# Cross-attention and quantised FFN: ScalarE's residual moved behind the gelu, TensorE's last products by tile behind four unused products, VectorE's affine passes half a step later

## The chip, the cores and the metric

The kernel runs on one core of a Trainium2 chip. The time is the device time of one launch in microseconds (us), the median of three executions. The engines are TensorE (PE for its matmuls, PEld for its weight loads), VectorE (DVE), ScalarE (ACT), GpSimd (POOL) and SyncE (SP), which here only issues transfers. Each engine takes its own instructions in order, and they meet through semaphores.

## What is computed

```
x = x + xattn(layernorm(x), ctx) @ Wo + bo          # x: 64 batches of 256 rows, 256 wide
h = bitlinear(layernorm(x) * g1 + b1n, W1, b1)      # 256 -> 1024, input rounded to 8 bits per row
h = gelu(h)
h = layernorm(h) * g2 + b2n                         # over the 1024
x = x + bitlinear(h, W2, b2)                        # 1024 -> 256, input rounded to 8 bits per row
...
bitlinear: scale = 127 / max|row|; round(row * scale) @ ternary(W).T / scale + b
```

## The kernel before

A batch is 256 rows, two tiles (t = 0, 1) of 128 rows. The program has two parts. The first (steps of `attn`) does the attention of all 64 batches (NB = 64) and the first layernorm of the FFN; it leaves the rounded rows of every batch turned in `h_t`. The second part (steps of `ffn`) does the rest of the FFN, and it alone is touched. Each engine has a function `ffn(j, n)` of its own, written by hand, that is called for j = 0, 1, 2, ...; the steps in the middle run in a hardware loop unrolled four times. The order within each `ffn` and the semaphores are all that sets the order of the work.

What happens to batch j, tile t:

- TensorE, `rows_up` (L1233, L1238): four matmuls of 512 columns and two more for the bias fill `u_p[t]`, two of the eight PSUM banks. There is one `u_p` for each tile, so batch j+1's tile t can be made only when ScalarE (`ssq_done`) and VectorE (`g_centred`) have read batch j's.
- ScalarE, `gelu` (L1089), in place in `u_p[t]`, with the row sum; `deviation`: the negative mean `g_nm` (L1094), the last 256 columns centred into `part` (L1097), and the sum of squares through a Square over all 1024 (L1099). An instruction with a row sum is followed by a short ACTIVATION_READ_ACCUMULATOR. After both tiles come `variance` (L1105) and, for batch j-2, `step_size` (L1110).
- VectorE, `centre` (L843): the first 768 columns, centred and times the gain, into `gn`. `affine` (L857): `gn` times the row's scale plus the offset, both tiles, 1024 columns each; the offset is read from PSUM banks 0 and 1 (`b2n_p`) from batch 4 on, before that from SBUF. `largest_rows` (L865): the largest magnitude of each row of both tiles.
- GpSimd, `gain_part` (L614): `part` times the gain; `scales` (L625): one power for the layernorm of j and the rounding scale of j-2; `quantise_batch` (L592, L597): rounds batch j-2 into `nq`; `store` (L588): issues the adding transfer of batch j-6 to the output.
- SyncE turns each rounded tile by a DMA transpose into `g_t` (L441).
- TensorE, `batch_down`: two steps after the rounding, 8 matmuls of 256 columns for each tile (L1267) into one PSUM bank for both tiles, and one correcting matmul (L1271).
- ScalarE, `residual` (L1129): takes those results out, one instruction of 256 columns a tile, batch j-5 in step j; every second step `bias_turned` (L1115) takes out the bias rows that TensorE turned (L1256).

The last four batches leave the loop: TensorE turns their rounded rows itself (L1261) and ScalarE copies them out (L1120).

## Time and profile before

| | |
|---|---|
| median of 3 executions | 1104.52 us (1102.41 to 1104.88) |
| profiled execution, its own time | 1107.87 us |
| its span, first to last instruction | 1106.2 us |
| busy share of the span: PE, DVE, ACT, POOL | 89%, 84%, 87%, 70% |
| TensorE's mean granted clock over the span | 0.919 of full |
| first part, until the first gelu | 590 us |
| second part, 64 batches | 516 us |

A row of the profile is one instruction or a group of like ones: when it started, how long it took, the engine, the line of the kernel, output and inputs. Brackets hold the idle time of the engine ahead of it and what ended it. The granted clock is the share of TensorE's full clock of 2.4 GHz that the chip let through; it has two levels, 1.0 and 0.5 (1.2 GHz), and a value between is a mean over a stretch with both.

### The profile page before, as it was taken

How to read it: one execution, taken by the hardware profiler on the slowest of the kernel's cores; microseconds unless marked ns; L12 is line 12 of the kernel's file. 1: busy time of each engine (PE TensorE's matmuls, PEld its weight loads, DVE VectorE, ACT ScalarE, POOL GpSimd, SP SyncE). 2: the span in 40 equal slices, each digit the busy share in tenths (PEclk: the TensorE clock that was granted, in tenths of full speed). 3: DMA queues.
4: the chain of work that ended last, by engine and by line, in shares of the span. 5: the costliest groups of instructions: out<-in, count | busy, mean ns of one | idle time of the engine just before them, and what ended most of it. 6: DMA issues, size and time to landing. Idle time of an engine off the chain costs nothing.

```text
span 1106.2 us, 25809 instructions
## 1 busy us (share of the span) xinstructions
PE 982.7 (89%) x7411; PEld 579.6 (52%) x7411; DVE 928.4 (84%) x1202; ACT 967.6 (87%) x2663; POOL 777.8 (70%) x1182
## 2 busy tenths in 40 slices
PE   6999999999999999999996688888888888888886
PEld 4666666666666666666662143434434344333344
DVE  2688788888888888888888988888898888898885
ACT  5889898989989889989977789999999999999994
POOL 3366566776666666666767767877887878788786
PEclk9999999999999999999998588888888888888889
DMA  6599978887878687866743257667666676676674
GB/s 175 134 176 195 177 154 168 158 167 160 163 170 167 162 157 166 159 167 173 155 106 101 57 82 109 98 102 113 99 101 105 96 110 100 101 111 99 103 107 74
DMA packets 271856, 145.93 MB, mean 132 GB/s; under 512 B 179097, under 2 KB 262297, under 8 KB 271793
## 3 DMA queue, kind: packets, MB, share of 16 engines
q1 hardware_dynamic: 254208, 128.24, 57.4%
q0 software_dynamic: 16864, 16.26, 12.7%
q8 instruction: 32, 0.52, 0.2%
q10 hardware_dynamic: 720, 0.66, 0.2%
q14 instruction: 32, 0.25, 0.1%
HBM read 71.62 MB, written 33.63 MB: 95 GB/s over the span
## 4 chain that ended last, share of the span: by engine, by line
PE 52%; ACT 20%; DVE 9%; issue 9%; DMA 5%; POOL 3%; SPq 1%; ACTq 1%; DVEq 0%; POOLq 0%
PE banks L1388 9%; PE banks L1379 8%; ACT banks L1089 8%; ACT g_dev L1099 7%; PE banks L1300 5%; PE banks L1267 5%; PE banks L1352 5%; PE banks L1341 4%; PE banks L1233 4%; DMA r_rows<-x_r 3%; PE banks L1372 3%; DVE g_max L865 2%; PE banks L1362 2%; PE banks L1238 2%; ACT part L1097 2%
## 5 line engine op out<-in xcount | busy, mean ns | idle before, releaser
L1233 PE MATMUL banks<-w_t,h_t 128*128 128x512 bf16 x504 | 149.8, 425 | 90.9 <-DVE gn_high L843 43.0
L1267 PE MATMUL banks<-w_t,g_t 128*128 128x256 bf16 x1024 | 167.1, 332 | 4.4 <-ACT h L1129 3.4
L1089 ACT ACTIVATE banks<-banks,h_dq 128x1024 f32<-128x1024 f32 x128 | 139.2, 1088 | 23.8 <-PE banks L1238 23.7
L759 DVE TRANSPOSE_TENSOR_REDUCE nm_part<-banks 128x64 f16<-128x2048 f32 x64 | 147.6, 2306 | 2.4 <-PE banks L1300 2.2
L1267 PEld LDWEIGHTS banks<-w_t,g_t 128*128 128x128 f16 x1024 | 114.2, 117 | 67.3 <-issue 32.4
L1042 ACT ACTIVATE probs<-banks 120x512 f32<-120x512 f32 x256 | 132.2, 603 | 17.9 <-PE banks L1330 14.5
L1099 ACT ACTIVATE g_dev<-banks,g_sum 128x1024 bf16<-128x1024 f32 x128 | 141.6, 1106 | 0.0
L1233 PEld LDWEIGHTS banks<-w_t,h_t 128*128 (+1 forms) x504 | 49.7, 105 | 174.6 <-issue 140.9
L1388 PE MATMUL banks<-wo_sb,o_t 128*128 128x256 f32 x512 | 137.2, 402 | 4.0 <-DVE o_t L779 3.7
L1379 PE MATMUL banks<-xt,wq_c 128*128 128x256 f32 x512 | 121.3, 380 | 0.0
L539 POOL COPY h_dq<-h_cl 128x2 f32<-128x2 f32 (+1 forms) x64 | 11.8, 184 | 140.8 <-DVE h_qs L822 139.8
L1388 PEld LDWEIGHTS banks<-wo_sb,o_t 128*128 128x128 f32 x512 | 87.8, 191 | 38.6 <-ACT log_sum L1031 25.4
L1379 PEld LDWEIGHTS banks<-xt,wq_c 128*128 128x128 f32 x512 | 92.5, 191 | 10.2 <-issue 0.2
L625 POOL TENSOR_TENSOR g_rq<-g_vm,powers 128x4 f32<-128x4 f32 x62 | 63.9, 1030 | 45.0 <-ACT g_vm L1110 45.0
L528 POOL TENSOR_TENSOR xr<-xr,bo_bc 128x512 f32<-128x512 f32 x64 | 81.7, 1276 | 18.1 <-DMA xr<-in_x 15.8
L1238 PE MATMUL banks<-bias_mov,bias_st 6*128 6x512 bf16 x252 | 85.7, 423 | 0.0
L857 DVE SCALAR_TENSOR_TENSOR gn_high<-gn_high,g_rq,banks 128x1024 f32<-128x1024 f32 x60 | 74.2, 1278 | 12.7 <-POOL g_rq L625 12.7
L843 DVE SCALAR_TENSOR_TENSOR gn_high<-banks,g_nm,g_bc 128x768 f32<-128x768 f32 x64 | 64.8, 1013 | 20.6 <-ACT g_dev L1099 19.5
L533 POOL TENSOR_TENSOR xr<-xr,b_bc 128x512 f32<-128x512 f32 x64 | 82.0, 1282 | 0.0
L857 DVE SCALAR_TENSOR_TENSOR gn_low<-gn_low,g_rq,banks 128x1024 f32<-128x1024 f32 x60 | 74.2, 1278 | 8.9 <-POOL g_rq L625 8.9
L843 DVE SCALAR_TENSOR_TENSOR gn_low<-banks,g_nm,g_bc 128x768 f32<-128x768 f32 x64 | 64.8, 1013 | 16.8 <-ACT g_dev L1099 12.4
L597 POOL TENSOR_SCALAR nq<-gn_low,g_rq 128x1024 f16<-128x1024 f32 x64 | 74.7, 1166 | 6.0
(172 smaller groups left out, 2506.1 us busy)
## 6 DMA issues: line engine op xcount, KB each, us to landing
x_in<-in_x SPq DMA_DIRECT2D x64, 256.0 KB
xt<-in_x_t SPq DMA_DIRECT2D x64, 256.0 KB, 5.4
xr<-in_x SPq DMA_DIRECT2D x64, 256.0 KB, 4.3
out<-xr SPq DMA_DIRECT2D x64, 256.0 KB, 7.0
...
```

The costliest lines, as they stand in the source:

```text
L533: pool.tensor_tensor(xr[:, r, :, :], xr[:, r, :, :], b2_bc[:, :].unsqueeze(1).to_broadcast([P, T, D]), ALU.add).then_inc(b2_done, 1)
L759: dve.tensor_reduce(nm_part[:, :, 0:C * RB], blocks_p, AX.X, ALU.max, negate=True, apply_transpose=True).then_inc(max_done, 1)
L843: dve.scalar_tensor_tensor(out=gn[n][:, t, 0:F - PART], in0=u_p[t][:, 0:F - PART], scalar=g_nm[:, n % 2, t:t + 1], in1=g2_bc[:, 0:F - PART ...
L857: dve.scalar_tensor_tensor(out=gn[n][:, t, :], in0=gn[n][:, t, :], scalar=g_rq[:, p, t:t + 1], in1=offset, op0=ALU.mult, op1=ALU.add).then ...
L1042: act.activation(probs[:, p, j, :, :], sc_p[0:KV, j, :, :], ACT.Exp, scale=SCALE).then_inc(probs_done, 1)
L1089: act.activation(u_p[t], u_p[t], ACT.Gelu, scale=h_dq[:, b, t:t + 1], accum_out=g_sum[:, p, t:t + 1]).then_inc(gelu_done, 1)
L1099: act.activation(g_dev[:, t, :], u_p[t], ACT.Square, scale=-float(F), bias=g_sum[:, p, t:t + 1], accum_out=g_ssq[:, p, t:t + 1]).then_inc( ...
L1233: pe.matmul(u_p[t][:, cols], h_t[:, b, t * C + c, :], w1_t[:, c, cols], start=(c == 0), stop=False, skip_group_check=True)
L1238: last = pe.matmul(u_p[t][:, cols], bias_st[k:k + NBIAS, n // 2, :], bias_mov[k:k + NBIAS, cols], start=False, stop=True, skip_group_check ...
L1267: pe.matmul(y[t], g_t[:, r, t, f, :], w2_t[:, f, :], start=(first and f == 0), stop=False, skip_group_check=True)
L1379: last = pe.matmul(q_p[:, m, :], wq_c[:, c, m * P:(m + 1) * P], xt[:, p, c, :], start=(c == 0), stop=(c == C - 1))
L1388: last = pe.matmul(y_p[:, t, :], o_t[:, p, c, t * P:(t + 1) * P], wo_sb[:, c, :], start=(c == 0), stop=(c == C - 1))
```

## The change

ScalarE's `ffn` puts `residual(j-5, t)` directly behind `gelu(j, t)`, ahead of the mean; the Square comes ahead of `part`; `bias_turned` moves from the end of the odd steps to the even steps, behind the second gelu; `step_size` comes ahead of `variance`.

TensorE does the down products by tile: `rows_up` tile 0, `rows_down` tile 0, `rows_up` tile 1, `rows_down` tile 1. Each `rows_down` first does four matmuls of the identity with `w2_t` (256 columns each) into the same PSUM words, which the real products overwrite. The two tiles' results now lie in banks 2 and 3, each with its own correcting matmul of 256 columns and its own count in `y2_ps`.

VectorE's `ffn(j)` is: `centre(j, 0)`, `affine(j-1)`, `centre(j, 1)`, `largest_rows(j-1)`. GpSimd's second `gain_part` comes behind `scales`. At the end, batches 60 and 61 are turned by DMA and taken by `rows_down`, and only 62 and 63 by TensorE.

ScalarE, the last steps of the second part (the same in the loop), before: gelu, mean, part, Square for each tile, then variance, step size and both residuals.

```order
L1089 ACTIVATE banks,g_sum<-banks,h_dq 128x1024
L1094 ACTIVATE g_nm<-g_sum 128x1
L1097 ACTIVATE part<-banks,g_nm 128x256
L1099 ACTIVATE g_dev,g_ssq<-banks,g_sum 128x1024
L1089 ACTIVATE banks,g_sum<-banks,h_dq 128x1024
L1094 ACTIVATE g_nm<-g_sum 128x1
L1097 ACTIVATE part<-banks,g_nm 128x256
L1099 ACTIVATE g_dev,g_ssq<-banks,g_sum 128x1024
L1105 ACTIVATE g_vm<-g_ssq 128x2
L1110 ACTIVATE g_vm<-g_max 128x2
L1129 ACTIVATE h<-banks,g_dq 128x256 x2
```

ScalarE there after the change (L1083 is the gelu, L1122 the residual, L1088 the mean, L1089 the Square, L1093 `part`).

```order
L1083 ACTIVATE banks,g_sum<-banks,h_dq 128x1024
L1122 ACTIVATE h<-banks,g_dq 128x256
L1088 ACTIVATE g_nm<-g_sum 128x1
L1089 ACTIVATE g_dev,g_ssq<-banks,g_sum 128x1024
L1093 ACTIVATE part<-banks,g_nm 128x256
L1083 ACTIVATE banks,g_sum<-banks,h_dq 128x1024
L1122 ACTIVATE h<-banks,g_dq 128x256
L1088 ACTIVATE g_nm<-g_sum 128x1
L1089 ACTIVATE g_dev,g_ssq<-banks,g_sum 128x1024
L1093 ACTIVATE part<-banks,g_nm 128x256
L1104 ACTIVATE g_vm<-g_max 128x2
L1099 ACTIVATE g_vm<-g_ssq 128x2
```

One residual now stands between each gelu and its mean, and nothing but two short instructions between the last `part` of a step and the next gelu.

TensorE, one of the last steps before, and after (L1226 and L1231 are `rows_up`, L1271 the four unused matmuls, L1260 the down products, L1262 the correction).

```order
L1233 MATMUL banks<-w_t,h_t 128x512 x4
L1238 MATMUL banks<-bias_mov,bias_st 128x512 x2
L1233 MATMUL banks<-w_t,h_t 128x512 x4
L1238 MATMUL banks<-bias_mov,bias_st 128x512 x2
L1267 MATMUL banks<-w_t,g_t 128x256 x16
L1271 MATMUL banks<-w_sum,neg_one 128x512
```

```order
L1226 MATMUL banks<-w_t,h_t 128x512 x4
L1231 MATMUL banks<-bias_mov,bias_st 128x512 x2
L1271 MATMUL banks<-w_t,ident_b 128x256 x4
L1260 MATMUL banks<-w_t,g_t 128x256 x8
L1262 MATMUL banks<-w_sum,neg_one 128x256
L1226 MATMUL banks<-w_t,h_t 128x512 x4
L1231 MATMUL banks<-bias_mov,bias_st 128x512 x2
L1271 MATMUL banks<-w_t,ident_b 128x256 x4
L1260 MATMUL banks<-w_t,g_t 128x256 x8
L1262 MATMUL banks<-w_sum,neg_one 128x256
```

The block of 17 down matmuls is cut into two of 13, one behind each tile of `rows_up`.

VectorE, one step before, and after (L839 is `centre`, L853 `affine`).

```order
L843 SCALAR_TENSOR_TENSOR gn_low<-banks,g_nm,g_bc 128x768
L865 TENSOR_REDUCE g_max<-gn_high 128x2
L843 SCALAR_TENSOR_TENSOR gn_low<-banks,g_nm,g_bc 128x768
L857 SCALAR_TENSOR_TENSOR gn_low<-gn_low,g_rq,banks 128x1024 x2
```

```order
L839 SCALAR_TENSOR_TENSOR gn_low<-banks,g_nm,g_bc 128x768
L853 SCALAR_TENSOR_TENSOR gn_high<-gn_high,g_rq,banks 128x1024 x2
L839 SCALAR_TENSOR_TENSOR gn_low<-banks,g_nm,g_bc 128x768
L865 TENSOR_REDUCE g_max<-gn_high 128x2
```

The affine pair now stands between the two centrings and is the previous batch's; the maximum stands at the end of the step.

The core of the diff:

```diff
 # GpSimd, ffn(j)
+                    scales(j, n % 2)
                     gain_part(j, 1, n)
-                    scales(j, n % 2)
                     quantise_batch(j - 2, (n + 2) % 4)
...
 # VectorE, ffn(j)
                     centre(j, 0, n)
+                    affine(j - 1, (n + 3) % 4)
+                    centre(j, 1, n)
                     largest_rows(j - 1, (n + 3) % 4)
-                    centre(j, 1, n)
-                    affine(j, n)
...
 # ScalarE, deviation
                     act.activation(g_nm[:, p, t:t + 1], g_sum[:, p, t:t + 1], ACT.Copy, scale=-1.0 / F).then_inc(gnm_done, 1)
+                    act.activation(g_dev[:, t, :], u_p[t], ACT.Square, scale=-float(F),
+                                   bias=g_sum[:, p, t:t + 1], accum_out=g_ssq[:, p, t:t + 1]).then_inc(ssq_done, 1)
                     after(act, part_done, (b - 2) * T + t + 1)
...
-                    act.activation(g_dev[:, t, :], u_p[t], ACT.Square, scale=-float(F),
-                                   bias=g_sum[:, p, t:t + 1], accum_out=g_ssq[:, p, t:t + 1]).then_inc(ssq_done, 1)
...
 # ScalarE, ffn(j)
+                    gelu(j, 0, p)
+                    if live(b, NB):
+                        residual(b, 0, (n + 3) % 4)
+                    deviation(j, 0, p)
+                    gelu(j, 1, p)
...
+                    if n % 2 == 0 and live(j + 2, NB) and not (isinstance(j, int) and j == 0):
+                        if live(b, NB):
+                            act.wait_ge(y2_ps, b * T + 2)
+                        bias_turned(j + 2, n // 2 ^ 1)
+                    if live(b, NB):
+                        residual(b, 1, (n + 3) % 4)
+                    deviation(j, 1, p)
+                    if live(j - 2, NB):
+                        step_size(j - 2, (n + 2) % 4)
                     variance(j, p)
...
 # TensorE
+                def rows_down(b, t, r):
+                    after(pe, out_done, (b - 1) * T + t + 1)
...
+                    pe.wait_ge(g_turned[r % 2], 16 * (b - r % 2) + 32)
+                    for f in range(FILL):
+                        pe.matmul(y2_tiles[t], ident_b[:, :], w2_t[:, f, :], start=True, stop=True)
+                    tile_down(b, t, r, y2_tiles[t]).then_inc(y2_ps, 1)
...
+                    if live(j + 1, NB):
+                        rows_up(j + 1, 0, (n + 1) % 4)
+                    if live(j - 4, NB):
+                        rows_down(j - 4, 0, n)
+                    if live(j + 1, NB):
+                        rows_up(j + 1, 1, (n + 1) % 4)
+                    if n % 2 == 1 and live(j + 3, NB):
+                        if live(j - 5, NB):
+                            pe.wait_ge(out_done, (j - 5) * T + T)
+                        turn_bias(j + 3)
+                    if live(j - 4, NB):
+                        rows_down(j - 4, 1, n)
...
 # TensorE, the end
+                for t in range(T):
+                    rows_down(NB - 4, t, 0)
...
+                turn_late(NB - 2, 0)
                 for t in range(T):
-                    turn_late(NB - 4, t)
...
+                    rows_down(NB - 3, t, 1)
+                turn_late(NB - 2, 1)
+                turn_late(NB - 1, 0)
                 pe.wait_ge(g_affine, NB * T)
                 for t in range(T):
...
+                    pe.wait_ge(gt_done, t + 1)
+                    tile_down(NB - 2, t, 2, y2_first[t]).then_inc(y2_ps, 1)
```

## Rows read from the trace of the kernel before

**Rows 1.** Stretches: PE, PEld, DVE, ACT, POOL busy (x instructions), granted clock, DMA share.

```profile
0.00:560.00 560.00, 543.51 (x5184) 367.73 (x5185) 458.92 (x786) 492.99 (x1538) 352.93 (x685) 1.00 0.79 165
645.44:1071.57 426.13, 351.09 (x1651) 167.14 (x1650) 369.76 (x280) 390.13 (x923) 342.45 (x391) 0.84 0.67 103
798.41:805.51 7.10, 5.00 (x29) 2.38 (x27) 5.28 (x5) 6.76 (x16) 4.53 (x6) 1.00 0.73 111
820.13:829.00 8.87, 8.48 (x31) 3.77 (x32) 8.03 (x7) 7.21 (x19) 7.62 (x10) 0.62 0.66 101
```

**Rows 2.** The gelu's line from 645 to 1072: count, durations, first and last start.

```profile
L1089 ACT ACTIVATE banks<-banks,h_dq x113: 1079/1087/1098, 645.4 to 1071.6; 128x1024 f32<-128x1024 f32 x113
```

**Rows 3.** Instructions in order of time, ScalarE, one step: start, duration, line.

```profile
804.59 0.20 ACT L1105 ACTIVATE g_vm<-g_ssq 128x2 f32<-128x2 f32 x1
...
804.79 0.83 ACT L1129 ACTIVATE h<-banks,g_dq 128x256 f32<-128x256 f32 x2
...
805.51 1.09 ACT L1089 ACTIVATE banks<-banks,h_dq 128x1024 f32<-128x1024 f32 x1
...
806.51 0.21 ACT L1089 ACTIVATION_READ_ACCUMULATOR banks<-banks,h_dq 128x1 f32 x1
...
806.75 0.20 ACT L1094 ACTIVATE g_nm<-g_sum 128x1 f32<-128x1 f32 x1
...
807.05 0.47 ACT L1097 ACTIVATE part<-banks,g_nm 128x256 f32<-128x256 f32 x1
...
807.42 1.11 ACT L1099 ACTIVATE g_dev<-banks,g_sum 128x1024 bf16<-128x1024 f32 x1
...
808.41 0.20 ACT L1099 ACTIVATION_READ_ACCUMULATOR g_dev<-banks,g_sum 128x1 f32 x1
808.51 1.09 ACT L1089 ACTIVATE banks<-banks,h_dq 128x1024 f32<-128x1024 f32 x1
...
812.01 0.28 ACT L1115 ACTIVATE bias_st<-banks 128x128 bf16<-128x128 f32 x1
```

**Rows 4.** The same view, VectorE, one step.

```profile
804.67 1.01 DVE L843 SCALAR_TENSOR_TENSOR gn_high<-banks,g_nm,g_bc 128x768 f32<-128x768 f32 x1
...
806.09 2.47 DVE L857 SCALAR_TENSOR_TENSOR gn_high<-gn_high,g_rq,banks 128x1024 f32<-128x1024 f32 x2 [0.41 <-POOL g_rq L625]
...
808.65 1.02 DVE L843 SCALAR_TENSOR_TENSOR gn_high<-banks,g_nm,g_bc 128x768 f32<-128x768 f32 x1
...
809.58 2.28 DVE L865 TENSOR_REDUCE g_max<-gn_high 128x2 f32<-128x2050 f32 x1
...
811.78 1.01 DVE L843 SCALAR_TENSOR_TENSOR gn_high<-banks,g_nm,g_bc 128x768 f32<-128x768 f32 x1
```

**Rows 5.** The same view, GpSimd's powers of two steps.

```profile
805.03 1.03 POOL L625 TENSOR_TENSOR g_rq<-g_vm,powers 128x4 f32<-128x4 f32 x1 [0.82 <-ACT g_vm L1110]
...
812.14 1.04 POOL L625 TENSOR_TENSOR g_rq<-g_vm,powers 128x4 f32<-128x4 f32 x1 [0.53 <-ACT g_vm L1110]
```

**Rows 6.** The same view, TensorE at full clock.

```profile
805.82 1.03 PE L1233 MATMUL banks<-w_t,h_t 128*128 128x512 bf16 x4 [1.53 <-DVE gn_high L843]
...
1057.23 1.04 PE L1233 MATMUL banks<-w_t,h_t 128*128 128x512 bf16 x4
...
1058.20 0.60 PE L1238 MATMUL banks<-bias_mov,bias_st 6*128 6x512 bf16 x2
...
1058.73 1.92 PE L1267 MATMUL banks<-w_t,g_t 128*128 128x256 bf16 x16
```

**Rows 7.** The same view, TensorE at half clock.

```profile
640.15 3.58 PE L1267 MATMUL banks<-w_t,g_t 128*128 128x256 bf16 x16
```

**Rows 8.** The same view, VectorE in the head of the second part.

```profile
600.52 3.78 DVE L857 SCALAR_TENSOR_TENSOR gn_low<-gn_low,g_rq,b2n_bc 128x1024 f32<-128x1024 f32 x2
...
605.36 1.01 DVE L843 SCALAR_TENSOR_TENSOR gn_low<-banks,g_nm,g_bc 128x768 f32<-128x768 f32 x1
```

**Rows 9.** The same view, the tail: GpSimd, then TensorE.

```profile
1095.07 1.11 POOL L597 TENSOR_SCALAR nq<-gn_high,last_scale 128x1024 f16<-128x1024 f32 x1
...
1096.69 1.04 PE L1267 MATMUL banks<-w_t,g_t 128*128 128x256 bf16 x8
```

201 lines of the change are left out of this document (74 added, 127 removed).

## Prediction

> **What bounds the kernel now.** I read the stretches first [rows 1]. In the first part PE is busy 543.51 of 560 us at full clock; the change doesn't touch it. The second part is another machine: from 645.44 to 1071.57 us ScalarE is busy 390.13 of 426.13, VectorE 369.76, GpSimd 342.45, and PE runs at a mean clock of 0.84. Its 113 gelus [rows 2] are 56 batches of two and the first of the next, so a batch costs 426.13 / 56 = 7.61 us. That mean hides two kinds of batch. One at full clock takes 7.10 us, with ScalarE busy 6.76 [rows 1]; one with the clock at 0.62 takes 8.87, with PE busy 8.48 of it. So there are two things to win: ScalarE's loop (VectorE's is nearly as long), and the batches in which TensorE's clock has fallen.
>
> Within a step at full clock I then read the starts, since a start to the next start is what an instruction costs its engine [rows 3]. ScalarE has no hole of size: gelu to gelu 805.51 to 808.51 is 3.00 us. But the mean starts 0.24 after the accumulator read, `part` 0.30 after the mean, and the variance waits likewise for the Square, where instructions that don't wait follow each other at 0.10. These are waits of an engine for its own results. VectorE [rows 4] is full as well but for 0.41 us in which the affine pair waits for GpSimd's power, which waits for the variance. GpSimd stands idle 0.53 us ahead of its power in a step of 7.11 [rows 5].
>
> **ScalarE after the change.** Old tile: 3.00, and for the batch 6.00, then to the variance, step size and both residuals and on to the next gelu 1.11: 7.11, as 798.41 to 805.51 shows. New tile, from the same rows: gelu to its read 1.00 (805.51 to 806.51), read to the next 0.10 (808.41 to 808.51), residual 0.36 (804.79 to 805.51 holds two), mean 0.10 with nothing left to wait for, Square to its read 1.00, read 0.10, `part` 0.37 (807.05 to 807.42). Sum 3.03. Batch: 6.06, and 0.20 for step size and variance: 6.26. The bias copy adds some 0.28 every second step: mean 6.40, against 7.11 plus 0.14 = 7.25. ScalarE gives up 0.85 us a batch. The cost of the move is at most 0.36 in latency to the Square and one more to `part`, of which more below.
>
> **VectorE.** Nothing is removed; the affine pair is only taken from behind the power. The loop is centre to next 0.93 (808.65 to 809.58), affine pair 2.56 (806.09 to 808.65), centre 0.93 again, maximum 2.20 (809.58 to 811.78) [rows 4]: 6.62 us. The power is now wanted after the next step's first centring, some 2 us after it is ready, so its 0.41 goes. What is late next is VectorE itself: 6.62 is above ScalarE's 6.40.
>
> **GpSimd.** The same instructions in another order. The step of 7.11 less 0.53 idle is 6.58 [rows 5], an upper bound, since small gaps for other waits are in it. It too lies at the new bound. The power now comes right behind the issue of `store`'s transfer, and the second gain behind the power; the affine pair that wants that gain comes a step later. SyncE has the same two transposes a batch, and two batches more at the end.
>
> **TensorE.** Added: 8 matmuls of 256 columns a batch. At full clock 16 such take 1.92 at most [rows 6], so 0.12 each, 0.96 a batch. The correction of 512 columns becomes two of 256, which is nothing. Half a step at full clock: `rows_up` from 1057.23 to 1058.73, 1.50; 12 matmuls of 0.12, 1.44; correction 0.12: 3.06, and 6.12 a batch, with some 0.1 for the bias turn 6.2. That is 93% of 6.62, so it does not bound, and in exchange its long holes go. At full clock it stood idle 1.53 us before a `rows_up` [rows 6] while all 17 down matmuls lay in one block; now each half step of 3.3 us holds 3.06 of work.
>
> **The clock.** It is this that decides. In the first part PE is busy 97% and the clock stays at 1.00 throughout; in the second the full-clock batch has PE busy 5.00 of 7.10, and the clock falls again and again [rows 1]. At half clock a down matmul takes 3.58 / 16 = 0.22 [rows 7]. With PE at 93% instead of 70% I expect the clock to stay at full from about batch 6 to batch 62. The fill is thus not free work in a hole: it is the price of 0.96 us of PE a batch, hidden only as long as the clock holds. At half clock a batch would be twice some 5.75, so 11.5 us, all PE, where the slow batch of before took 8.87.
>
> **New waits.** ScalarE's residual of batch j-5 now waits for down products that PE makes right behind `rows_up` of batch j, the very products the gelu ahead of it waited for. If ScalarE was starved, the gelu takes 1.10 and the down products 1.56: the residual waits some 0.5 with the mean, the Square and VectorE's centring queued behind it. Is the whole ring then longer than 6.62? Centring to `rows_up` 1.15 (804.67 to 805.82), `rows_up` 1.50, fill and down 1.56, a guess of 0.25 for the end of the last matmul and the semaphore, residual 0.36, mean 0.10, Square with its read 1.20, to the centring 0.05: 6.17 us. It is shorter than VectorE's loop by 0.45, so the wait is absorbed. I take 6.75 us a batch: 6.62, and 0.13 for jitter between four engines at 6.2 to 6.6.
>
> **Head, tail and sum.** Steady part: 56 batches by 7.61 - 6.75 = 0.86: -48 us. With 6.62 it is -55. Head: the first affine pair took 3.78 us where a later one takes 2.47, and held back the next centring [rows 8]; it moves behind it, a gain of 1 to 4 us. Against it stand the fills at half clock in the first two down steps, 8 by 0.22 each, 3.5 us in all. I take 0, between -4 and +4. The Trainium skill (SBUF — State Buffer, section "SBUF: two separate sides") says that a VectorE instruction with two SBUF inputs and a GpSimd one that reads SBUF shut each other out; the slow pair does read its offset from SBUF and the fast one reads it from PSUM, so trace and page agree. By that rule the new overlaps of the steady part cost nothing, since no instruction there has two SBUF inputs. Tail: GpSimd's chain to the rounding of batch 63's first tile (1095.07, [rows 9]) is the same length, but TensorE now makes 62's first tile behind its transpose instead of ahead: +1.1 us, 8 down matmuls of 1.04. Sum against the profiled execution: 1107.87 - 48.2 + 1.1 = 1060.8; that execution lies 3.35 above the median, so **1057 us**.
>
> **The rivals.** (a) The forecast, clock at full and VectorE's loop the bound: 1046 (6.62 a batch and a good head) to 1068. Chance 0.72.
>
> (b) The new ring binds: the wait of 0.5 at each residual isn't absorbed. ScalarE's 6.40 becomes 7.25 with 0.43 twice. For it speaks that PE has 7% to spare and the residual waits on it directly; against it the ring of 6.17. 1105.6 - 56 by 0.36 = 1085. Chance 0.12.
>
> (c) The clock falls now and then, say 15% of the time: 0.85 / 6.75 + 0.15 / 11.5 batches per us is 7.19 us a batch, 1082. Chance 0.07.
>
> (d) The other side: the clock falls as often as before. A mean of 0.84 is 32% of the time at half clock; 0.68 / 6.75 + 0.32 / 11.5 gives 7.78 us a batch, 9 us more in all than before: 1115. It decides from 27% on (there the batch is 7.61). The place is the fill, which makes each fall dearer. Against it stand the short holes. The Trainium skill (TensorE: Matmul & The Clock Gate, section "A second HAM failure mode: psum-queue depth-cycling") tells of a kernel whose clock went up and down although its pauses between groups of matmuls were small; by that rule this is what would happen. Before the change the trace bears it out only with holes of 1.5 us. Chance 0.06.
>
> (e) ScalarE's waits on itself aren't shortened and the clock changes nothing: 1104.5. Chance 0.03.
>
> **How the numbers follow.** (a) and the lower part of (b) and (c) lie under 1086: with 0.72, 0.07 and most of 0.12 the range 1046 to 1086 holds over 0.8. A measurement can tell 0.2% here, 2.2 us. Faster: (a), (b), (c) = 0.91. Same: 0.03. Slower: (d) = 0.06.
>
> **What would show it.** Right: gelu to gelu of a tile 6.6 to 6.8 us; the clock 1.00 in all stretches from 650 to 1070; VectorE with no idle time ahead of the affine pair; idle time of PE below 0.6 us at each `rows_up`; the mean 0.1 behind the residual. Wrong: ScalarE idle ahead of the residual by 0.4 us at every tile (b), half-clock stretches with PE over 95% busy (c, d), GpSimd with no idle time ahead of its power and VectorE waiting for it, in which case GpSimd's 6.58 was the bound and nearly the same time comes for another reason.

## The result and the profile after

| | before | after |
|---|---|---|
| median, range | 1103.55 us (1102.41 to 1104.88, 4 executions) | 1044.30 us (1041.61 to 1046.85, 4 executions) |
| ratio | 1 | 0.9462 (0.9433 to 0.9492) |
| profiled execution, its span | 1107.87, 1106.2 us | 1043.15, 1041.5 us |
| mean granted clock over the span | 0.919 | 0.980 |
| batch, mean of batches 6 to 61 | 7.61 us | 6.63 us |

The kernel became 5.4% faster. The forecast was 1057 us; the time lies 1.7 us below the range. Faster was right, and so was the place. But the fill (the four unused products ahead of each tile's down products), by which the prediction meant to hold the clock, turned out to be ballast. What failed is the bound of a batch, put at 6.75 us and measured at 6.63, and the head, put at 0 and measured at -3.4 us.

Ratios, here and below, leave out executions that lie over 1.5% above the fastest of their kernel, while medians hold them all; that concerns one of four of b_fill8, three of ten of selfwaits_fill0 and one of before that took 3100.59 us.

Of the profiled span of before, 64.7 us are gone. Four stretches hold them:

| stretch | before | after | difference |
|---|---|---|---|
| until the first gelu | 589.97 | 584.50 | -5.5 |
| head: batches 0 to 5 | 55.47 | 52.10 | -3.4 |
| batches 6 to 61 | 426.13 | 371.21 | -54.9 |
| tail, from batch 62's gelu | 34.63 | 33.69 | -0.9 |

The first row isn't the change's: the first part is untouched and took 584 to 596 us in the profiled executions of all kernels run here. Before's profiled execution lay 4.3 us above its median and after's 1.15 below, 5.5 together. The other three sum to 59.2 us, the difference of the medians (59.25).

The same three stretches of after, in the view by windows (length, then busy time of PE, PEld, DVE, ACT, POOL with instructions, granted clock, DMA share, GB/s):

```profile
584.50:636.60 52.10, 37.21 (x119) 13.18 (x118) 47.49 (x67) 38.63 (x93) 33.13 (x41) 0.64 0.27 61
636.60:1007.81 371.21, 347.40 (x2156) 188.78 (x2155) 365.40 (x280) 361.06 (x926) 338.98 (x392) 1.00 0.76 118
1007.81:1041.50 33.69, 26.45 (x213) 19.18 (x210) 24.50 (x26) 17.57 (x45) 26.09 (x30) 0.95 0.80 124
```

Against the second line of [rows 1] the clock stands at 1.00 instead of 0.84, and VectorE is busy 98% instead of 87%. The page's clock row shows one dip only, at the start of the second part:

```profile
PEclk9999999999999999999999958999999999999999
```

ScalarE in one step of after (instructions in order of time: start, duration, line; L1083 gelu, L1122 residual, L1088 mean, L1089 Square, L1093 `part`), from tile 1's gelu on. It answers to [rows 3]:

```profile
805.39 1.13 ACT L1083 ACTIVATE banks<-banks,h_dq 128x1024 f32<-128x1024 f32 x1
806.39 0.25 ACT L1083 ACTIVATION_READ_ACCUMULATOR banks<-banks,h_dq 128x1 f32 x1
806.73 0.47 ACT L1122 ACTIVATE h<-banks,g_dq 128x256 f32<-128x256 f32 x1
807.10 0.19 ACT L1088 ACTIVATE g_nm<-g_sum 128x1 f32<-128x1 f32 x1
807.20 1.10 ACT L1089 ACTIVATE g_dev<-banks,g_sum 128x1024 bf16<-128x1024 f32 x1
808.19 0.20 ACT L1089 ACTIVATION_READ_ACCUMULATOR g_dev<-banks,g_sum 128x1 f32 x1
808.29 0.47 ACT L1093 ACTIVATE part<-banks,g_nm 128x256 f32<-128x256 f32 x1
...
813.38 0.28 ACT L1109 ACTIVATE bias_st<-banks 128x128 bf16<-128x128 f32 x1 [0.18 <-PE banks L1262]
813.56 0.47 ACT L1122 ACTIVATE h<-banks,g_dq 128x256 f32<-128x256 f32 x1
813.91 0.20 ACT L1088 ACTIVATE g_nm<-g_sum 128x1 f32<-128x1 f32 x1
814.01 1.11 ACT L1089 ACTIVATE g_dev<-banks,g_sum 128x1024 bf16<-128x1024 f32 x1
815.00 0.21 ACT L1089 ACTIVATION_READ_ACCUMULATOR g_dev<-banks,g_sum 128x1 f32 x1
815.10 0.48 ACT L1093 ACTIVATE part<-banks,g_nm 128x256 f32<-128x256 f32 x1
```

The mean now follows the residual by 0.37, the residual's own time, and the Square follows the mean by 0.10: those waits of ScalarE for itself are gone. What it waits for instead is TensorE. The residual at 806.73 starts 0.34 behind the accumulator read, where 0.10 is usual, since the correction of its tile ends only at 806.63 (next fence but one); the bias copy waits 0.18.

VectorE (L839 centring, L853 affine, L865 maximum; [rows 4]), then TensorE (L1226 and L1231 `rows_up`, L1271 fill, L1260 down, L1262 correction; [rows 6]):

```profile
802.38 1.02 DVE L839 SCALAR_TENSOR_TENSOR gn_high<-banks,g_nm,g_bc 128x768 f32<-128x768 f32 x1 [0.21 <-ACT part L1093]
...
805.58 1.02 DVE L839 SCALAR_TENSOR_TENSOR gn_high<-banks,g_nm,g_bc 128x768 f32<-128x768 f32 x1
806.51 2.46 DVE L853 SCALAR_TENSOR_TENSOR gn_high<-gn_high,g_rq,banks 128x1024 f32<-128x1024 f32 x2
808.89 1.01 DVE L839 SCALAR_TENSOR_TENSOR gn_high<-banks,g_nm,g_bc 128x768 f32<-128x768 f32 x1
...
815.61 1.02 DVE L839 SCALAR_TENSOR_TENSOR gn_low<-banks,g_nm,g_bc 128x768 f32<-128x768 f32 x1
```

```profile
803.54 1.03 PE L1226 MATMUL banks<-w_t,h_t 128*128 128x512 bf16 x4 [0.50 <-DVE gn_high L839]
804.51 0.60 PE L1231 MATMUL banks<-bias_mov,bias_st 6*128 6x512 bf16 x2
805.04 0.61 PE L1271 MATMUL banks<-w_t,ident_b 128*128 128x256 bf16 x4
805.49 1.04 PE L1260 MATMUL banks<-w_t,g_t 128*128 128x256 bf16 x8
806.36 0.27 PE L1262 MATMUL banks<-w_sum,neg_one 128*128 128x256 bf16 x1
...
810.04 1.03 PE L1226 MATMUL banks<-w_t,h_t 128*128 128x512 bf16 x4 [0.21 <-DVE gn_high L839]
...
812.92 0.27 PE L1262 MATMUL banks<-w_sum,neg_one 128*128 128x256 bf16 x1
...
816.77 1.03 PE L1226 MATMUL banks<-w_t,h_t 128*128 128x512 bf16 x4 [0.26 <-DVE gn_low L839]
```

The holes of 1.53 us ahead of `rows_up` [rows 6] have shrunk to 0.5 at most. And **the ring closes in these three fences**. Tile 1's `rows_up` at 803.54, the end of its down products at 806.63, residual 806.73, mean 807.10, Square 807.20, `part` 808.29, centring 808.89, next `rows_up` of tile 1 at 810.04: 6.50 us. The next turn has the bias copy in it: 810.04, correction from 812.92, bias copy 813.38, residual 813.56, Square 814.01, `part` 815.10, centring 815.61, `rows_up` 816.77: 6.73. The mean of the two is 6.62; a batch takes 6.63. Every link of the second turn waits for the one before it. In the first only the centring at 808.89 stands behind something else, VectorE's affine pair, by 0.09: 1.69 from the Square's start, where it is 1.60 in the second turn.

So the bound is the ring that the prediction put at 6.17, not VectorE, which idled 5.7 us of the 350 between 650 and 1000 us. The experiments had to say whether that reading is right.

### The profile page after: what moved, and what is told of

It is laid out like the page before. It is cut to its first block, busy times and chain, and to the rows that moved or that the text cites. A ratio compares the mean times of both kernels' runs of the same rounds, so it can differ in the third digit from the quotient of the medians.

```text
span 1041.5 us, 27013 instructions
## 1 busy us (share of the span) xinstructions
PE 980.9 (94%) x7938; PEld 606.5 (58%) x7938; DVE 921.4 (88%) x1202; ACT 933.0 (90%) x2659; POOL 769.6 (74%) x1182
## 4 chain that ended last, share of the span: by engine, by line
PE 63%; DVE 17%; issue 9%; ACT 6%; DMA 2%; POOL 1%; DVEq 0%; ACTq 0%; SPq 0%; POOLq 0%
PE banks L1382 11%; PE banks L1373 9%; PE banks L1294 6%; PE banks L1346 5%; PE banks L1335 5%; PE banks L1226 5%; DVE g_max L865 5%; PE banks L1260 4%; DVE gn_low L853 4%; DVE gn_high L853 4%; PE banks L1366 3%; PE banks L1356 2%; PE banks L1231 2%; PE banks L1271 2%; PE banks L1324 2%
## 5 line engine op out<-in xcount | busy, mean ns | idle before, releaser
L1226 PE MATMUL banks<-w_t,h_t 128*128 128x512 bf16 x504 | 137.8, 398 | 35.5 <-DVE gn_low L839 19.6
L1083 ACT ACTIVATE banks<-banks,h_dq 128x1024 f32<-128x1024 f32 x128 | 140.9, 1101 | 11.7 <-PE banks L1231 11.1
L1089 ACT ACTIVATE g_dev<-banks,g_sum 128x1024 bf16<-128x1024 f32 x128 | 142.8, 1115 | 0.0
L1260 PE MATMUL banks<-w_t,g_t 128*128 128x256 bf16 x1024 | 134.4, 275 | 0.7 <-ACT g_t L1114 0.7
L1260 PEld LDWEIGHTS banks<-w_t,g_t 128*128 128x128 f16 x1024 | 100.9, 99 | 13.2 <-ACT g_t L1114 0.9
L1226 PEld LDWEIGHTS banks<-w_t,h_t 128*128 (+1 forms) x504 | 47.9, 99 | 97.5 <-issue 68.5
L527 POOL TENSOR_TENSOR xr<-xr,bo_bc 128x512 f32<-128x512 f32 x64 | 81.6, 1275 | 13.9 <-DMA xr<-in_x 11.6
L1271 PE MATMUL banks<-w_t,ident_b 128*128 128x256 bf16 x496 | 76.5, 277 | 3.4 <-ACT h L1122 3.4
L1231 PE MATMUL banks<-bias_mov,bias_st 6*128 6x512 bf16 x252 | 78.8, 393 | 0.0
L587 POOL DMA_DIRECT2D out<-h x62 | 78.0, 1263 | 0.6 <-ACT h L1122 0.5
L1294 PE MATMUL banks<-q_t,k_t 32*128 32x256 f32 x1024 | 73.3, 400 | 2.9 <-ACT probs L1036 1.5
L596 POOL TENSOR_SCALAR nq<-gn_low,g_rq 128x1024 f16<-128x1024 f32 x64 | 71.6, 1119 | 6.0
L853 DVE SCALAR_TENSOR_TENSOR gn_high<-gn_high,g_rq,banks 128x1024 f32<-128x1024 f32 x60 | 74.0, 1273 | 0.0
```

What stands on the lines that cost most here:

```text
L853: dve.scalar_tensor_tensor(out=gn[n][:, t, :], in0=gn[n][:, t, :], scalar=g_rq[:, p, t:t + 1], in1=offset, op0=ALU.mult, op1=ALU.add).then ...
L1083: act.activation(u_p[t], u_p[t], ACT.Gelu, scale=h_dq[:, b, t:t + 1], accum_out=g_sum[:, p, t:t + 1]).then_inc(gelu_done, 1)
L1089: act.activation(g_dev[:, t, :], u_p[t], ACT.Square, scale=-float(F), bias=g_sum[:, p, t:t + 1], accum_out=g_ssq[:, p, t:t + 1]).then_inc( ...
L1226: pe.matmul(u_p[t][:, cols], h_t[:, b, t * C + c, :], w1_t[:, c, cols], start=(c == 0), stop=False, skip_group_check=True)
L1231: last = pe.matmul(u_p[t][:, cols], bias_st[k:k + NBIAS, n // 2, :], bias_mov[k:k + NBIAS, cols], start=False, stop=True, skip_group_check ...
L1260: pe.matmul(y, g_t[:, r, t, f, :], w2_t[:, f, :], start=(f == 0), stop=False, skip_group_check=True)
```

## The experiments

The table holds all kernels; "batch" is the mean over batches 6 to 61 of the profiled execution, and "clock" its granted clock between 650 and 1000 us. For b_fill8 the profiled execution is the slowest of four, for selfwaits_fill0 the third slowest of ten, so most of their other executions have shorter batches. Kernels are named by whether they have the orders of after ("a_", or "fill0_" where the fill is out too) or of before ("b_"). The cuts of code show the main lines of an edit; "..." stands for lines left out.

| kernel | median, us | ratio to before (95%) | batch | clock |
|---|---|---|---|---|
| a_fill0 | 1036.10 | 0.9358 (0.9291 to 0.9425) | 6.43 | 1.00 |
| b_fill8 | 1138.83 | 1.0226 (1.0145 to 1.0308) | 8.30 | 0.81 |
| a_selfwaits | 1128.11 | 1.0188 (1.0152 to 1.0225) | 7.99 | 1.00 |
| a_dveold | 1071.50 | 0.9669 (0.9626 to 0.9712) | 7.01 | 1.00 |
| a_again | 1048.10 | 0.9457 (0.9426 to 0.9489) | 6.63 | 1.00 |
| fill0_again | 1039.54 | 0.9369 (0.9338 to 0.9400) | 6.43 | 1.00 |
| a_fill2 | 1044.47 | 0.9420 (0.9376 to 0.9464) | 6.52 | 1.00 |
| b_split | 1252.30 | 1.1314 (1.1258 to 1.1370) | 10.08 | 0.67 |
| a_max768 | 1045.53 | 0.9430 (0.9384 to 0.9476) | 6.63 | 1.00 |
| fill0_dveplus | 1044.41 | 0.9402 (0.9358 to 0.9447) | 6.58 | 1.00 |
| fill0_partfirst | 1067.25 | 0.9609 (0.9558 to 0.9660) | 6.98 | 1.00 |
| selfwaits_fill0 | 1127.17 | 1.0117 (1.0067 to 1.0166) | 8.12 | 0.92 |
| b_split2 | 1165.41 | 1.0489 (1.0446 to 1.0531) | 8.55 | 0.71 |
| b_sqfirst | 1078.02 | 0.9716 (0.9676 to 0.9756) | 7.03 | 0.90 |
| fill0_head | 1037.80 | 0.9345 (0.9309 to 0.9382) | 6.43 | 1.00 |

### Does the fill hold the clock?

The theory of the prediction was yes. The rival: the clock holds since no engine waits long any more, and the fill only costs TensorE time. **a_fill0** leaves the unused products out of after.

```diff
-    FILL = 4
+    FILL = 0
```

> The changed kernel without the four unused matmuls ahead of each tile's down products. Theory A (the fill holds the clock): TensorE's work falls from some 6.2 us a batch to 5.2 of 6.63, its holes grow by about 0.5 us each half step, the clock falls again for 15 to 30% of the steady part, a batch costs about 7.1 us and the kernel 1060 to 1085 us. Theory B (the split by tile alone holds the clock, and the fill is ballast): clock 1.00 from batch 6 to 62, 6.63 us a batch, 1044 us.

**b_fill8** puts eight of them into before, ahead of each batch's down products, and changes nothing else.

```diff
                     pe.wait_ge(g_turned[r % 2], 16 * (b - r % 2) + 32)
+                    for f in range(FC):
+                        pe.matmul(y2_tiles[0], ident_b[:, :], w2_t[:, f, :], start=True, stop=True)
                     for t in range(T):
```

> The kernel before with eight unused matmuls ahead of each batch's 16 down products and nothing else changed. Theory A: the clock stays at full, the batches of 8.87 us go, ScalarE's loop of 7.25 us a batch is left: 1103.5 - 56 x 0.36 = 1083 us. Theory B (only the orders matter, the clock would have done no harm without them): 8 more matmuls on TensorE gain nothing, 1104 to 1115 us.

The stretch from 650 to 1000 us by windows: before, after, a_fill0, b_fill8.

```profile
650.00:1000.00 350.00, 289.63 (x1357) 137.83 (x1355) 303.19 (x230) 320.08 (x757) 281.50 (x322) 0.84 0.67 103
```

```profile
650.00:1000.00 350.00, 327.46 (x2031) 178.22 (x2028) 344.30 (x264) 339.92 (x871) 319.35 (x370) 1.00 0.76 118
```

```profile
650.00:1000.00 350.00, 290.18 (x1659) 141.35 (x1657) 350.00 (x274) 348.24 (x897) 330.62 (x382) 1.00 0.78 122
```

```profile
650.00:1000.00 350.00, 314.68 (x1575) 165.54 (x1575) 278.64 (x212) 295.31 (x698) 257.89 (x295) 0.81 0.61 95
```

Without the fill PE is busy 290.18 us, 83%, and the clock is 1.00 all the same. With the fill in before PE is busy 314.68 us and the clock is 0.81, but that is the slowest of its four executions. Over the whole span the granted clock was 0.898 in it and 0.912 to 0.923 in the other three, where before had 0.915 to 0.919 in seven executions on that chip. So the fill didn't raise the clock of before; that it lowered it isn't shown. The kernel is 2.3% slower (1.5 to 3.1%). In these two orders the theory fails both ways: the clock holds without the fill, and falls with it. (A third order, in selfwaits_fill0 below, speaks for it.) What the fill does in after is to cost 0.20 us a batch, 11 us over 56. To be sure of it I ran after and a_fill0 again on one chip, and the fill at half size.

> The changed kernel itself, on the same chip as the next three. Both theories: 1044 us, 6.63 us a batch.

> The changed kernel without the unused matmuls once more, beside the changed kernel. Theory C (the fill sits in the ring of centring, rows up, fill, down products, residual, mean, Square, part, and that ring bounds the changed kernel at 6.63 us; without the fill VectorE's loop of 6.43 bounds): 6.43 us a batch and 10 to 12 us less in all, ratio to the changed kernel 0.989. Theory D (the gain seen once was drift between executions): within 3 us of the changed kernel.

> The changed kernel with two unused matmuls instead of four ahead of each tile's down products. Theory C: the ring is shorter by 2 x 0.11 = 0.22 us, which brings it to VectorE's loop: 6.43 to 6.5 us a batch, 1034 to 1037 us. Theory E (TensorE's own load costs, 0.05 us a batch for each unused matmul of a tile): 6.53 us a batch, 1039 us.

They gave 1048.10, 1039.54 and 1044.47 us, and batches of 6.63, 6.43 and 6.52. The fill costs 8.6 us on the same chip, and half of it about half. The last run came out as theory E had it (6.53), not theory C. With a ring of 6.62 less 0.22, VectorE's 6.43 should bound, but in the trace the centring behind VectorE's maximum starts up to 2.37 us after it, where 2.19 is the least, so something still holds VectorE up in some steps. Why the batch is 6.52 stays open; what bounds the kernel with the whole fill and with none is tested further down.

### Which parts bring the gain?

**a_selfwaits** gives ScalarE its waits on itself back in after: residual ahead of the gelu, `part` ahead of the Square, and VectorE's centring waits for the Square.

```diff
+                    if live(b, NB):
+                        residual(b, 0, (n + 3) % 4)
                     gelu(j, 0, p)
-                    if live(b, NB):
-                        residual(b, 0, (n + 3) % 4)
                     deviation(j, 0, p)
...
```

> The changed kernel with ScalarE's waits on itself put back: the residual stands ahead of the gelu, so the mean follows the gelu at once, and part stands between the mean and the Square; VectorE's centring waits for the Square again. Same work everywhere, fill and split kept. Theory A (ScalarE's loop would bind again): clock 1.00, about 7.1 to 7.25 us a batch, 1044 + 56 x 0.55 = 1075 us. Theory B (the clock alone made the gain and VectorE bounds at 6.62 either way): 1044 to 1050 us.

It took 7.99 us a batch, 1.36 more than after, where the prediction put 0.85 on ScalarE's whole gain. There is a side effect that I had not seen: with the residual ahead of it the gelu too waits for the down products, and the ring is longer by a gelu. The run says nothing on the waits alone. What it does show is a clock of 1.00 at 7.99 us a batch (0.977 to 0.980 over the whole span in all four executions).

**a_dveold** keeps after's ScalarE and TensorE and takes VectorE's and GpSimd's orders of before.

```diff
                     centre(j, 0, n)
-                    affine(j - 1, (n + 3) % 4)
-                    centre(j, 1, n)
                     largest_rows(j - 1, (n + 3) % 4)
+                    centre(j, 1, n)
+                    affine(j, n)
```

> The changed kernel with VectorE's and GpSimd's orders of the kernel before (affine of batch j at the end of step j, behind the power). Fill, split and ScalarE's order kept. Theory A (VectorE's loop of 6.62 us bounds, and the wait for the power comes on top of it): idle time of 0.4 to 1.0 us ahead of each affine pair, 7.0 to 7.6 us a batch, about 1078 us (1065 to 1100). Theory B (the place of the affine pair is nothing, the wait is hidden by slack elsewhere): 1044 us.

7.01 us a batch with the clock at 1.00. So in this kernel of the 0.98 us of the steady part 0.60 come without the new orders of VectorE and GpSimd and 0.38 with them. The head took 55.05 us here, as before's 55.47, against 52.10 in after: the head's gain comes with VectorE's and GpSimd's new order too.

**fill0_partfirst** repeats a cleaner half of a_selfwaits without the fill: only `part` ahead of the Square, and the centring behind the Square as in before. **selfwaits_fill0** is all of a_selfwaits without the fill.

```diff
                     act.activation(g_nm[:, p, t:t + 1], g_sum[:, p, t:t + 1], ACT.Copy, scale=-1.0 / F).then_inc(gnm_done, 1)
-                    act.activation(g_dev[:, t, :], u_p[t], ACT.Square, scale=-float(F),
-                                   bias=g_sum[:, p, t:t + 1], accum_out=g_ssq[:, p, t:t + 1]).then_inc(ssq_done, 1)
...
+                    act.activation(g_dev[:, t, :], u_p[t], ACT.Square, scale=-float(F),
+                                   bias=g_sum[:, p, t:t + 1], accum_out=g_ssq[:, p, t:t + 1]).then_inc(ssq_done, 1)
```

> The changed kernel without unused matmuls, with part ahead of the Square as in the kernel before (the centring waits for the Square). Theory H (the order saves ScalarE a wait of 0.20 us for its own mean in each tile): ScalarE's loop goes from 6.40 to 6.8, above VectorE's 6.43: 6.8 us a batch, 1038 + 56 x 0.37 = 1059 us. Theory I (the wait is hidden, VectorE bounds either way): 1038 us.

> The run with ScalarE's waits on itself put back (residual ahead of the gelu, part ahead of the Square), now without the unused matmuls. The ring there is centring, rows up, down products, residual, gelu, mean, part, Square; it measured 7.99 us with the fill. Theory F (the length of TensorE's holes sets the clock): TensorE has no more work than in the kernel before, in batches at least as long, but cut in two; holes near 1 us, clock 1.00, and a batch 4 x 0.11 = 0.44 us shorter than with the fill, 7.55 us: 1128 - 25 = 1103 us. Theory G (TensorE's share of the time sets it): some 5.2 us of work in 7.55 is the share of the kernel before, the clock falls as there, mean 0.84, 8.2 us a batch or more, 1140 us.

The order of those two instructions is worth 0.55 us a batch in the changed kernel without the fill (6.98 against 6.43), more than the 0.37 expected. The other run took 1112.62 to 1149.07 us in ten executions. Its batches at full clock take 7.61 us, near the 7.55 expected, but in its trace the clock fell at different places, for two to eight batches at a time, to a mean of 0.92.

That run differs from a_selfwaits by the fill alone, and it is the one pair that supports the prediction's view of the fill. With the fill the granted clock over the whole span was 0.977 to 0.980 in four executions; without it, 0.919 to 0.959 in ten. It still brings no time: what the higher clock gains the longer ring loses, and against before the two kernels stand at 1.0188 and 1.0117.

**b_sqfirst** makes the same swap in before, and nothing else: the Square ahead of `part`, the centring waits for `part`.

```diff
-                    dve.wait_ge(ssq_done, j * T + t + 1)
+                    dve.wait_ge(part_centred, j * T + t + 1)
...
```

> The kernel before with the Square ahead of part (the centring waits for part), nothing else. Theory H (ScalarE's loop loses 2 x 0.20 us of waits for its own mean): but the centring starts 0.15 to 0.37 us later, VectorE's affine pair stands behind it and waits for the power, and VectorE is nearly as long: 0.1 to 0.3 us a batch less at full clock, and the slow batches as they are, 1095 to 1103 us. Rival (the clock rules the kernel before, and the self-waits are hidden): 1108 us.

ScalarE in it, one tile (L1095 is now the Square, L1099 `part`):

```profile
834.54 1.10 ACT L1089 ACTIVATE banks<-banks,h_dq 128x1024 f32<-128x1024 f32 x1
835.53 0.22 ACT L1089 ACTIVATION_READ_ACCUMULATOR banks<-banks,h_dq 128x1 f32 x1
835.79 0.20 ACT L1094 ACTIVATE g_nm<-g_sum 128x1 f32<-128x1 f32 x1
835.90 1.10 ACT L1095 ACTIVATE g_dev<-banks,g_sum 128x1024 bf16<-128x1024 f32 x1
836.89 0.19 ACT L1095 ACTIVATION_READ_ACCUMULATOR g_dev<-banks,g_sum 128x1 f32 x1
836.99 0.46 ACT L1099 ACTIVATE part<-banks,g_nm 128x256 f32<-128x256 f32 x1
837.34 1.09 ACT L1089 ACTIVATE banks<-banks,h_dq 128x1024 f32<-128x1024 f32 x1
...
839.78 0.47 ACT L1099 ACTIVATE part<-banks,g_nm 128x256 f32<-128x256 f32 x1
840.13 0.20 ACT L1105 ACTIVATE g_vm<-g_ssq 128x2 f32<-128x2 f32 x1
```

The Square needs `g_sum`, not the mean, and starts 0.11 behind it, where `part` started 0.30 behind it in [rows 3]. A tile takes 2.80 us instead of 3.00. A third wait goes too: the variance (L1105) stood right behind the Square's read, 0.29 from its start (804.30 to 804.59 in before); now `part` lies between them and the variance follows it by 0.35, `part`'s own time. That is 2 x 0.20 and 0.19, 0.59 us in all, and before's 30 batches at full clock average 7.20 us where this kernel's 44 average 6.61. Both expectations missed by far (0.1 to 0.3 us a batch, or nothing): they left out the variance and took VectorE for a second bound. That swap alone takes 32.8 us off the kernel (1110.80 to 1078.02), more than half of what the whole change brings. One of its batches at full clock by windows:

```profile
834.54:841.24 6.70, 5.11 (x30) 2.66 (x30) 6.56 (x6) 6.64 (x18) 6.27 (x9) 1.00 0.77 117
```

Its full-clock batches are as short as after's 6.63. Only its twelve batches with a fallen clock, 7.4 to 9.4 us, bring the mean to 7.03. So the rest of the change, on top of this swap and with the fill in, makes no batch at full clock shorter: what it goes with is a clock that holds. 7.03 less 6.63, by 56, is 22 us, of the 28 or so by which after beats this kernel (ratios 0.9462 and 0.9716). Before lost as much to its clock: 7.61 less 7.20, by 56, is 23 us.

### What bounds the batch?

**a_max768** makes VectorE's maximum shorter in after by leaving out the first 256 columns. **fill0_dveplus** adds a memset of 256 columns a step to VectorE where the fill is out.

```diff
-                    dve.tensor_reduce(g_max[:, n, :], gn_floored[n], AX.X, ALU.max,
+                    dve.tensor_reduce(g_max[:, n, :], gn_floored[n][:, :, PART:F + 1], AX.X, ALU.max,
```

```diff
                     largest_rows(j - 1, (n + 3) % 4)
+                    dve.memset(spare[:, :], 0.0)
```

> The changed kernel with its fill; the maximum leaves out the first 256 columns of each row, which is 2 x 256 columns or 0.53 us less on VectorE a batch. Theory C (with the fill the ring through TensorE bounds at 6.6): 6.50 to 6.63 us a batch, 1040 to 1046 us. Theory J (VectorE's loop bounds with the fill too): the batch falls to ScalarE's 6.40, 1033 us.

> The changed kernel without unused matmuls, with one memset of 128 x 256 more on VectorE in each step. Theory C (without the fill VectorE's loop bounds): each microsecond more on VectorE is one more a batch; 0.25 to 0.33 us a batch, +14 to +18 us: 1054 us. Rival (the ring or ScalarE bounds at 6.43 and VectorE waits for them): under +5 us.

VectorE in a_max768:

```profile
801.60 1.02 DVE L839 SCALAR_TENSOR_TENSOR gn_high<-banks,g_nm,g_bc 128x768 f32<-128x768 f32 x1 [0.29 <-ACT part L1093]
802.53 1.74 DVE L865 TENSOR_REDUCE g_max<-gn_low 128x2 f32<-128x1538 f32 x1
804.79 1.02 DVE L839 SCALAR_TENSOR_TENSOR gn_high<-banks,g_nm,g_bc 128x768 f32<-128x768 f32 x1 [0.52 <-ACT part L1093]
```

The maximum takes 1.74 instead of 2.28 us, and VectorE waits for `part` just as much longer: 6.63 us a batch, unchanged. VectorE doesn't bound the changed kernel. Where the fill is out it does: a_fill0 has it busy 350.00 of 350 us, and fill0_dveplus pays 0.15 us a batch for a memset of 0.19. (The 0.25 to 0.33 expected had the memset too dear.) Its loop, from a_fill0:

```profile
801.47 1.01 DVE L839 SCALAR_TENSOR_TENSOR gn_high<-banks,g_nm,g_bc 128x768 f32<-128x768 f32 x1
802.39 2.28 DVE L865 TENSOR_REDUCE g_max<-gn_low 128x2 f32<-128x2050 f32 x1
804.59 1.01 DVE L839 SCALAR_TENSOR_TENSOR gn_high<-banks,g_nm,g_bc 128x768 f32<-128x768 f32 x1
805.51 2.47 DVE L853 SCALAR_TENSOR_TENSOR gn_high<-gn_high,g_rq,banks 128x1024 f32<-128x1024 f32 x2
807.89 1.02 DVE L839 SCALAR_TENSOR_TENSOR gn_high<-banks,g_nm,g_bc 128x768 f32<-128x768 f32 x1
```

801.47 to 807.89 is 6.42 us, with the affine pair at 2.38 to the next start. The fill makes the ring longer by 0.45 (805.04 to 805.49 in after); without it the ring would be some 6.2 (an estimate: 6.62 less 0.45), and VectorE's 6.43 takes over. So the fill costs 0.20 and not 0.45.

### What makes the clock hold?

**b_split** cuts before's block of 17 down products in two, one half behind each tile of `rows_up`, with the other orders as in before and no fill, but for the bias copy, which stands behind the first gelu of the even steps. It is built from after. To keep it from waiting, tile 1 of a batch is made half a step later than tile 0. TensorE's step, without the tests for the first and last batches and the waits:

```diff
+                        rows_up(j + 1, 0, (n + 1) % 4)
+                        rows_down(j - 5, 1, (n + 3) % 4)
...
+                        rows_up(j + 1, 1, (n + 1) % 4)
...
+                        rows_down(j - 4, 0, n)
```

> The split of the down products alone: tile 0's stand behind the second rows up and tile 1's of the batch before behind the first, no unused matmuls; ScalarE's order within a step (gelu, mean, part, Square, both residuals at the end), VectorE's and GpSimd's are those of the kernel before. Theory F (what lets the clock fall is the hole of 1.5 to 1.9 us in TensorE's work, not its total): holes below 1 us, clock 1.00 from batch 6 on, ScalarE's loop of 7.11 to 7.25 us a batch, 1103.5 - 56 x 0.4 = 1080 us. Theory G (the clock holds only where batches are short, because then TensorE's share of the time is higher): the clock falls as before, 7.6 us a batch, 1100 us.

It was 13% slower than before, where 1080 or 1100 us had been expected, by a wait that my edit had made: ScalarE's residual of tile 1 waited for TensorE, 77.0 us of 350.

```profile
ACT h L1124 <- PE banks L1261: 77.0, 33, 2.7
```

**b_split2** takes that residual half a step later, behind tile 0's Square.

```diff
                     deviation(j, 0, p)
+                    if live(j - 6, NB):
+                        residual(j - 6, 1, (n + 2) % 4)
                     gelu(j, 1, p)
```

> The cut of the down products alone, all other orders within a step those of the kernel before, no unused matmuls; unlike b_split the residual of batch j-6's tile 1 stands behind the Square of tile 0 in step j and that of j-5's tile 0 at the end, so that neither waits for products just issued. Theory F (short holes hold the clock): holes of 1 us or less but for the bias turns, clock 1.00 in most of the steady part, ScalarE's loop of 7.11 to 7.25 us binds, 1108 - 56 x 0.36 = 1088 us. Theory G (TensorE's share of the time decides, and it is that of the kernel before): the clock falls as before, 7.6 us a batch, 1108 us.

It was still 4.9% slower, at a clock of 0.71, with holes of up to 2.6 us ahead of `rows_up` that before doesn't have. This edit too brings waits of its own: behind each bias turn TensorE waits for ScalarE to have copied it (11.6 us of 350), and that copy stands idle for 23.5 us. So neither run is the cut alone. Whether the cut by itself holds the clock or gains anything isn't shown.

**fill0_head** asks the question for the head, where the clock is low in every kernel: eight unused products behind each `rows_up` of batches 1 to 4, none elsewhere.

```diff
+                    if isinstance(b, int) and b <= 4:
+                        for f in range(FC):
+                            pe.matmul(bank[2][:, 0:D], ident_b[:, :], w2_t[:, f, :], start=True, stop=True)
```

> The changed kernel without unused matmuls in the steady part, but with eight behind each rows up of batches 1 to 4, in the head of the second part, where TensorE stands idle for 2 to 5 us at a time. Theory K (the half clock bounds the head: rows up takes 2.9 us instead of 1.5 in a ring with both tiles): the clock stays or comes back earlier, 5 to 10 us less, 1030 us. Rival (VectorE's and GpSimd's work bounds the head, and the unused matmuls stand in the way of the next rows up): 1038 to 1045 us.

The head by windows, a_fill0 and then fill0_head:

```profile
589.68:640.47 50.79, 34.91 (x109) 12.22 (x108) 46.92 (x66) 38.53 (x94) 33.04 (x41) 0.66 0.31 63
```

```profile
590.46:641.95 51.49, 38.30 (x170) 18.01 (x172) 47.28 (x66) 38.63 (x93) 33.21 (x41) 0.80 0.28 62
```

Here unused work did raise the clock, from 0.66 to 0.80, and the head got no shorter. VectorE is busy 92% of it; a faster TensorE has nothing to give there.

I looked for one number that sorts the kernels by clock. Two don't (where nothing is said, the share is that of 650 to 1000 us):

| kernel | clock | PE's share of busy time | longest wait ahead of `rows_up` |
|---|---|---|---|
| before | 0.84 | 70% in a full-clock batch | 1.5 us |
| b_sqfirst | 0.90 | 76% in a full-clock batch | 1.5 us |
| b_fill8 | 0.81 | 82% in its full-clock batches | 1.5 us |
| selfwaits_fill0 | 0.92 | 69% in its full-clock batches | 1.9 us |
| fill0_partfirst | 1.00 | 75% | 1.5 us |
| a_selfwaits | 1.00 | 78% | 1.4 us |
| a_fill0 | 1.00 | 83% | 0.7 us |
| after | 1.00 | 94% | 0.5 us |

fill0_partfirst holds full clock with PE's share below and its longest wait hardly shorter than those of b_fill8, which doesn't (1.47 against 1.53 us). All that the runs show is that with after's order of TensorE's work, down products behind each tile's `rows_up`, the clock stayed up in nine of ten kernels (all but selfwaits_fill0), with the fill and without, and that in the kernels with all down products in one block it fell. The two splits, which fell too, had orders of their own and long waits. Neither ScalarE's swap (b_sqfirst, fill0_partfirst) nor VectorE's order (a_dveold) decides it. **What exactly sets the clock stays open.**

## Why the prediction was right or wrong

**Right: ScalarE's waits on itself.** The prediction saw starts 0.24 and 0.30 us apart where 0.10 is usual, and gave ScalarE 6.40 us a batch without them. ScalarE is busy 348.24 us of 350 in a_fill0 at 6.43. b_sqfirst shows that `part`'s and the variance's waits are worth over half of the whole change.

**Right: VectorE's wait for the power.** The affine pair has no idle time ahead of it in after. a_dveold prices the move at 0.38 us a batch on top of the rest; the wait was 0.41. Without the rest it isn't needed for short batches: b_sqfirst has VectorE's old order and 6.61 at full clock.

**Right in effect, wrong in cause: the clock.** It stayed at 1.00 from batch 6 on, as forecast, and that is worth some 23 us of 54.9, less than half of the steady gain. But that the clock decides, and the fill as the means of holding it, are refuted for these orders by b_sqfirst, a_fill0 and b_fill8; only a_selfwaits beside selfwaits_fill0 shows a clock that the fill holds. The step that failed took the share of busy time as the cause because the first part, at 97%, and the second, at 70%, differed in it. They differ in much else. The sentence from the Trainium skill (TensorE: Matmul & The Clock Gate, section "A second HAM failure mode: psum-queue depth-cycling") on a clock that goes up and down although its pauses are small stood for rival (d), and its outcome, 1115 us, didn't come. The runs neither show that mechanism nor exclude it: the kernels whose clock fell had pauses of 1.5 us and more ahead of `rows_up`, and fill0_partfirst with 1.5 us held.

**Wrong: the bound, VectorE at 6.62 instead of the ring, by two errors that nearly cancelled.** The affine pair was put at 2.56 from its start to the next (806.09 to 808.65 in [rows 4]). The next instruction was a centring that waited for ScalarE's Square, whose accumulator read started at 808.41 [rows 3]: the pair itself takes 2.38. VectorE's loop is 6.43, not 6.62. And the ring was put at 6.17, with "Square with its read 1.20, to the centring 0.05". But the centring in after waits for `part`, which now stands behind the Square: 1.60 from the Square's start (800.78 to 802.38, 814.01 to 815.61), 0.35 more. The bias copy of every second step, 0.18 of it in the ring, and TensorE's bias turn were left out too. The ring is 6.62. That is rival (b)'s mechanism, at a bound that happens to equal the one I gave to VectorE. That the forecast's 6.62 came was luck.

**Wrong: 0.13 for jitter.** There is none. The batches of after repeat in a cycle of four, and their mean is the ring's sum within 0.02. This is the largest single miss: 0.12 by 56 is 6.7 us.

**Mis-sized: the head.** Forecast 0, between -4 and +4; measured -3.4. The gain from the new place of the affine pair came (a_dveold, without it, took 55.05). Of the 3.5 us for the fills at half clock a_fill0's head of 50.79 shows 1.3, where VectorE is busy 47.49 us of 52.10. The reading of the slow pair was too simple, though. The prediction set 3.78 us with the offset in SBUF against 2.47 with it in PSUM. But before has four pairs with the offset in SBUF, of 3.78, 2.47, 4.03 and 2.46 us. Two of them, and GpSimd beside them:

```profile
610.21 2.47 DVE L857 SCALAR_TENSOR_TENSOR gn_low<-gn_low,g_rq,b2n_bc 128x1024 f32<-128x1024 f32 x2
618.67 4.03 DVE L857 SCALAR_TENSOR_TENSOR gn_high<-gn_high,g_rq,b2n_bc 128x1024 f32<-128x1024 f32 x2
...
611.56 1.70 POOL L614 TENSOR_TENSOR gn_high<-part,g_bc 128x256 f32<-128x256 f32 x1 [1.95 <-ACT part L1097]
```

So the offset's place alone doesn't make a pair slow. Where the pair started first, GpSimd's product took 1.70 us instead of 0.72; where GpSimd's rounding had started first (618.45), the pair took 4.03. In after the four pairs take 11.0 us together instead of 12.7, so they give 1.7 of the head's 3.4; the rest wasn't traced.

**Mis-sized: the tail.** Forecast +1.1; measured -0.9. From batch 63's first gelu to the start of the last addition it did get longer, by 1.9 (22.59 to 24.47). But batch 62 was shorter by 0.6, and the span now ends 2.2 us after the last addition where it ended 4.5 after it. The first and the last of the four last additions, VectorE:

```profile
1034.62 0.48 DVE L955 SCALAR_TENSOR_TENSOR h<-banks,g_dq,xr 128x256 f32<-128x256 f32 x1 [4.01 <-PE banks L1262]
...
1038.79 0.48 DVE L955 SCALAR_TENSOR_TENSOR h<-banks,g_dq,xr 128x256 f32<-128x256 f32 x1 [1.74 <-PE banks L1262]
```

What made the last transfer shorter wasn't tried.

**The sum.** The forecast missed by 12.7 us: 6.7 in the steady part, 3.4 in the head, 2.0 in the tail, and 1.0 because before's median, with a fourth execution, was 1103.55; rounding gives 0.4 back. The range's lower end, 1046, was 6.62 a batch and a good head, and both came. It had nothing below that for the tail, whose end was held to be known, and nothing for the base.

**A version better than both** is the changed kernel without the unused products: 1036.10 and 1039.54 us in two runs, 6.4% and 6.3% faster than before. There VectorE is busy without a pause and ScalarE 99.5%, so the next gain has to come from the work of both.
